# Turning xf ahead of the second branch's high products, and the router's first layer and x1's transposes ahead of its low ones

## What is computed

```
h  = softmax(x xT / 16) x                      # inside each tile
h  = h + xn + circular convolution, decayed scan over time, correlation   (xn = layernorm(h))
xf = layernorm(h)
router: logits = gelu(xf W1r + b) W2r + b      # two of eight experts for each row
twice: ctx = [x, v]; shared and two routed experts: gelu(ctx w1 + b) w2 + b -> gates, halt
refined = gelu(x2 r1 + b) r2 + b
out = h + xf + weight * refined
```

## Time and profile before

| | us |
|---|---|
| median of 3 runs | 774.84 (774.31 to 776.21) |
| the profiled execution | 774.78 |
| its span, first to last instruction | 773.0 |

### The profile page before, as it was taken

The page is one execution under the profiler, slowest core; times in us unless marked ns, Lnnn a source line. Parts: engine busy times, 40 slices in busy tenths (PEclk is TensorE's granted clock), DMA queues, the critical chain, the costliest instruction groups (busy, mean ns, idle before and its releaser), DMA issues.

```text
span 773.0 us, 14304 instructions
## 1 busy us (share of the span) xinstructions
PE 728.1 (94%) x4516; PEld 615.8 (80%) x4516; DVE 610.8 (79%) x1430; ACT 569.3 (74%) x1359; POOL 372.1 (48%) x438
## 2 busy tenths in 40 slices
PE   5757999999999999999999999999999999999986
PEld 3646778888888888888888888888888888888875
DVE  4847778978978878878878878879789789789662
ACT  4665778787787787887887886887887887877663
POOL 1426446445555555545545555454564564463310
PEclk9688999999999999999999999999999999999997
DMA  8300000000000000000000000000000000000000
GB/s 326 123 15 1 8 0 12 10 21 3 19 22 2 21 21 3 20 22 0 22 22 1 22 22 1 21 22 1 22 21 1 8 8 2 8 8 1 8 8 14
DMA packets 11611, 17.27 MB, mean 22 GB/s; under 512 B 1232, under 2 KB 10504, under 8 KB 11024
## 3 DMA queue, kind: packets, MB, share of 16 engines
q1 hardware_dynamic: 11536, 16.35, 6.2%
HBM read 13.20 MB, written 3.15 MB: 21 GB/s over the span
## 4 chain that ended last, share of the span: by engine, by line
PE 66%; ACT 15%; DVE 12%; issue 5%; POOL 1%; DMA 1%; SPq 0%; POOLq 0%; ACTq 0%; DVEq 0%
PE ctl L495 23%; PE ctl L511 10%; PE ctl L472 5%; PE ctl L501 4%; PE ctl L514 4%; ACT L906 4%; ACT L1060 3%; DVE both L1324 3%; DVE work L1319 3%; PE cd L472 3%; PE cd L666 3%; PE ctl L481 3%; ACT work L909 2%; DVE both L1325 2%; PE ctl L482 2%
## 5 line engine op out<-in xcount | busy, mean ns | idle before, releaser
L375 POOL TENSOR_TENSOR hm_lo<-gl,mexp 128x256 fp32r<-128x256 f32 x144 | 127.8, 913 | 124.2 <-DVE gl L1256 120.7
L495 PE MATMUL ctl<-w2e_hi,hm_hi 128*128 128x512 f32 (+1 forms) x432 | 160.9, 382 | 0.1
L495 PE MATMUL ctl<-w2e_lo,hm_hi 128*128 128x512 f32 (+1 forms) x432 | 150.3, 360 | 0.0
L965 ACT ACTIVATE work<-ctl 128x256 f32<-128x256 f32 (+1 forms) x144 | 70.2, 487 | 68.6 <-PE ctl L514 59.1
L1242 DVE TENSOR_TENSOR hm_hi<-ge,mexp 128x256 fp32r<-128x256 f32 x144 | 88.7, 631 | 20.0 <-ACT ge L946 17.7
L495 PEld LDWEIGHTS ctl<-w2e_hi,hm_hi 128*128 128x128 f32 x432 | 82.1, 190 | 24.7 <-DVE hm_hi L1242 8.0
L511 PE MATMUL ctl<-w2e_hi,hm_lo 128*128 128x512 f32 (+1 forms) x432 | 100.0, 357 | 0.0
L495 PEld LDWEIGHTS ctl<-w2e_lo,hm_hi 128*128 128x128 f32 x432 | 82.3, 191 | 10.5
L511 PEld LDWEIGHTS ctl<-w2e_hi,hm_lo 128*128 128x128 f32 x432 | 74.6, 188 | 13.6 <-POOL hm_lo L375 0.2
L381 POOL TENSOR_TENSOR rg_lo<-rg,rg_hi 128x512 fp32r<-128x512 f32 x23 | 37.7, 1639 | 70.8 <-ACT rg_hi L902 70.8
L967 ACT ACTIVATE work<-ctl 128x256 f32<-128x256 f32 x144 | 54.5, 378 | 0.0
(11 more groups left out here) (211 smaller groups left out, 2040.3 us busy)
## 6 DMA issues: line engine op xcount, KB each, us to landing
work<-params_dram SPq DMA_DIRECT2D x3, 1152.0 KB, 13.2
xT<-turned_dram SPq DMA_DIRECT2D x24, 128.0 KB, 2.2
out_dram<-y SPq DMA_DIRECT2D x24, 128.0 KB, 1.7
xa<-x_dram SPq DMA_DIRECT2D x16, 128.0 KB, 2.2
par<-params_dram SPq DMA_DIRECT2D x1, 1280.0 KB, 10.9
work<-params_dram SPq DMA_DIRECT2D x2, 512.0 KB, 11.2
xa<-x_dram SPq DMA_DIRECT2D x8, 119.0 KB
par<-params_dram SPq DMA_DIRECT2D x1, 512.0 KB, 16.0
```

The lines of the kernel that those rows point to most:

```text
L375: TT(hm[1][:, j, c, :], gl[:, c, part, :], pairs(tile, j, c), ALU.mult).then_inc(done, 1)
L495: mm(dst[:, a:z], hm[0][:, j, c, :], w2e[i][:, c, a:z], start=(c == 0 and i == 0), stop=False)
L965: AF(tan[tile.s][:, 1:kinds, j, :], ctl_t[:, D:kinds * D].rearrange("p (a d) -> p a d", a=kinds - 1), ACT.Tanh, scale=0.5)
```

## The change

Only the order of steps in two `slot` functions changes; no instruction is added or removed, and every step keeps its own waits.

On PE, xf's transposes (L686 in the new numbering) come directly behind `refine_in(o)`, ahead of `expert_hi` of the second routed branch. The router's first layer and `turned(n)` then come ahead of `expert_end` and `expert_lo` of that branch. On ACT, the two copies of xf come ahead of `refine_units(o)`, and the two copies of x1 ahead of `unit(t, 2)`.

```diff
@@ PE's slot @@
                 if o.exists() and t.exists():
                     refine_in(o)
 
+                if f.exists():
+                    passed(pe, xf_v, f)
+                    for q in range(KD):
+                        last = nc.tensor.transpose(pd[:, q * P:(q + 1) * P], xf[f.s][:, q * P:(q + 1) * P], ident)
+                    last.then_inc(xfT_ps, 1)
+
                 if t.exists():
                     passed(pe, hm1_v, t, per=3)
                     passed(pe, u1_sb, t, per=BR, step=1)
                     if t.low == 0:
                         pe.wait_ge(set_dve, 3)
                     expert_hi(ctl[0], 1, t, hm1_v, 0, 2 * D)
-
-                if f.exists():
-                    passed(pe, xf_v, f)
-                    for q in range(KD):
-                        last = nc.tensor.transpose(pd[:, q * P:(q + 1) * P], xf[f.s][:, q * P:(q + 1) * P], ident)
-                    last.then_inc(xfT_ps, 1)
-
-                if t.exists():
-                    expert_end(ctl[0], 1, t, en1_v, 2 * D)
-                    expert_lo(ctl[0], 1, t, hl1_g, eb1_sb, u1_ps, 2 * D)
 
                 if f.exists():
                     passed(pe, xfT_sb, f)
...
                     turned(n)
+
+                if t.exists():
+                    expert_end(ctl[0], 1, t, en1_v, 2 * D)
+                    expert_lo(ctl[0], 1, t, hl1_g, eb1_sb, u1_ps, 2 * D)
 
                 if f.exists():
                     passed(pe, rh_sb, f)
@@ ACT's slot @@
                     unit(t, 1, u1_sb, u1_ps, ctl[1], 2)
 
+                if f.exists():
+                    passed(act, e_ps, f, back=1, per=2)
+                    passed(act, rh_ps, f, back=1)
+                    passed(act, xfl_g, f, back=1)
+                    state(xfT, pd, D, f, xfT_ps, xfT_sb)
+                    state_hi(1, pd, f, xfh_sb, f)
+
                 if o.exists():
...
                     refine_units(o)
 
                 if f.exists():
-                    passed(act, e_ps, f, back=1, per=2)
-                    passed(act, rh_ps, f, back=1)
-                    passed(act, xfl_g, f, back=1)
-                    state(xfT, pd, D, f, xfT_ps, xfT_sb)
-                    state_hi(1, pd, f, xfh_sb, f)
                     passed(act, rh_ps, f)
                     AF(rh[:, :], pd[0:HID, 0:P], ACT.Gelu, bias=pv("b1r", HID)).then_inc(rh_sb, 1)
...
-                if t.exists():
-                    unit(t, 2, u1_sb, u1_ps, ctl[0], 2)
-
                 if n.exists() and t.exists():
...
                         state_hi(0, pc, n, x1h_sb, f)
+
+                if t.exists():
+                    unit(t, 2, u1_sb, u1_ps, ctl[0], 2)
```

## The result

The changed kernel takes 792.57 us (median of 4 runs, 789.78 to 793.13); the kernel before, on the same chip, 774.58 (4 runs, 772.30 to 776.21). The ratio is 1.0227 (95% interval 1.0191 to 1.0263): 18 us slower, where 9.6 were forecast, and above the range. The profiled execution took 792.92 us, its span 791.1, the mean granted clock 0.974 as before.

A forecast was written before the change was run, and what follows sets the result against it. PE was busy for 94% of the span; the slot's end was taken as set by ACT and DVE, PE's path some 0.2 us shorter. 774.8 + 5.0 (middle slots) + 3.1 (first slots) + 1.5 (clock) = 784.4 us, range 778.8 to 789.8.

The forecast's parts named there:

- rival (a): Whole kernel: slower, as worked out, 784.4 us with a range of 778.8 to 789.8; chance 0.82.
- the stall: PE at xf's transposes, middle slots: free at 390.66, it waits for DVE's xf until 391.27, 0.61 us idle.
- Rival (b): PE at xf's transposes: faster, 771.4 us, as PE begins the high products during the wait for xf; chance 0.04.
- The step that failed: DVE's routing steps behind L717: 0.44 us later, held to be outside the chain of waits, which goes over ACT.
- rival (d): Much slower, 794 us: POOL's `rg_lo` late for PE, or table loads pushed further, 0.5 us a slot more; chance 0.07.
- +0.25 a slot: Middle slots: PE's way grows by 0.44 - 0.19, ACT's by 0.11, so PE is later; 20 slots, +5.0 us.
- the wait at L481 should be nearly gone: PE at L481, before `sab`: a sign expected in the changed profile; PE's 0.19 us there is given back.
- rival (c): No change: PE's loss is given back where it meets DVE or ACT, as at L481; 776.5 us; chance 0.07.
- The first slots: Slots of tiles 0 to 2: high products come behind the wait for xf; together +3.1 us, from +2 to +3.5.
- one fall: PE's clock in tiles 1 and 2: one longer idle gap brings half speed, +1.5 us; none to two, 0 to +3.5.

The follow-up runs named there:

- experiment 6: Parts of the change alone in the kernel before: only xf's transposes early, 793.09 us; only low products and `unit(t, 2)` late, 790.70; only ACT's new order, 795.40.
- experiment 1: Changed kernel with POOL's u0 and `vu` subtractions ahead of its two additions into `base`: 783.85 us, ratio 1.0108 to the kernel before.
- experiment 8: Changed order from tile 3 on only, with POOL's u0 and `vu` ahead of `base`: 779.41 us, ratio 1.0050 to the kernel before.
- experiment 4: Changed kernel with the new order only from tile 3 on, tiles 0 to 2 keeping the old one: 785.56 us, ratio 1.0124 to the kernel before.
- experiment 2: Kernel before with POOL's u0 and `vu` ahead of `base`: 775.87 us, ratio 1.0000.
- experiment 5: Changed kernel with xf's transposes behind four of the six high products instead of ahead of all: 788.72 us, ratio 1.0185 to the kernel before.
- experiment 3: Kernel before with one more 128x128 addition, its result unused, on POOL in each slot: 779.52 us, ratio 1.0039.

## Why the prediction was right and wrong

**Right:** slower (rival (a)), with the stall it named. The transposes start at 6.94 us where PE was free at 6.34: 0.60 for the 0.61 forecast. The waits at L686 are 15.7 us in 24 slots (some 13 forecast), those of L717 for `rh` are gone, ACT idles ahead of the copies of xf. Rival (b) fell: PE held the high products behind the transposes that waited, in every slot. `rg_hi` and POOL's `rg_lo` are early enough, as worked out; L381 takes even less (1295 ns for 1639): before, it stands beside DVE's L1314 (392.44 to 393.39) in tile 12 and takes 1.69, after, beside no DVE instruction, 1.29.

**The step that failed** is the sentence "DVE's routing steps begin 0.44 later with L717; they were not in the chain of waits, which goes over ACT." They are what POOL's four instructions wait for, and these shut out DVE's product on the way to `sab`. That made 0.31 of the slot's 0.49, 6 us. The measured time is close to rival (d)'s 794, but by luck: the half of (d) that named a later table load was not it (the load is 0.18 later, near the 0.11 forecast), and PE did not wait for `rg_lo`. The collision could be read from before: POOL's L425 took 1.45 us next to 0.74 for its twin L421, and DVE's L1324 1.11 next to 0.69 for L1325. I looked at POOL only for what PE waits for.

**The term "+0.25 a slot".** PE's steps came to 4.42 for the forecast 4.27: 0.19 from the transposes to the first high product (0.13 forecast) and 0.32 from L514 to L717 (0.25). So L562 is 0.58 later (0.44). But more could be given back than 0.19. I had taken 0.58 for the pitch from L742 to L481, and 0.36 is possible (experiment 6), so at least 0.41 was to spare there (0.77 - 0.36), and 0.15 more at `hm_hi` (10.68 from L481 to the next slot before, 10.53 after). PE's own way therefore ends at 29.54 at most and does not set the slot. What does, once the sum no longer meets POOL, is ACT's way, with DVE's as long: 0.18 for the 0.11 forecast, as `unit(t, 2)` waits for the later L514. So the 0.25 was near the 0.18 that experiments 1 and 8 show, but it was put on the wrong engine, and that is luck. With the collision it is 0.49: 9.7 us for the forecast 5.0.

**The end of the slot in the kernel before.** I took the 0.17 us of idle time at L481 for ACT's and DVE's one way. They are two, and the later one passes through `hm_hi`. This is why "the wait at L481 should be nearly gone" failed (7.5 us in 23 waits), and why rival (c), which looked for all that is given back at L481, looked in one of two places.

**The first slots.** +3.1 and one fall, +1.5, were forecast; measured +6.8, and 7.0 by experiment 4. Tile 0 has +1.34 (1.15), tile 2 0.97 without its fall (0.98). The second fall, 1.5, was in the range of the term. Tile 1's +3.0 is 1.0 for the order, 1.5 for its fall and 0.5 for the longer slow stretch at its start, which no term had.

**The sum:** 5.0 + 3.1 + 1.5 were forecast, 9.7 + 6.8 came, and 1.5 ahead of tile 0 that the order doesn't explain. The range ended at 789.8, with 0.40 a slot as its upper bound; 0.49 with the collision is beyond that, and experiment 1, where the sum doesn't meet POOL, is inside with 783.85. One sum of the prediction is wrong in itself: rival (c) with 0.1 a slot and +1 gives 774.8 + 2 + 1 = 777.8, not 776.5; this changes no other number.

## What to carry to other kernels

Ask of every step that moves not only who waits for it, but which instructions of DVE and POOL will then stand side by side: two instructions of one shape on one engine that differ in length (1.45 and 0.74, 1.11 and 0.69) mark a collision that no wait shows. Idle time ahead of a matmul can be missing as well: whether it waited is told by its start against the end of what it needs. Before costing an order, write the slot as the largest of its ways, each with its margin; two such sums did it here, and they showed that the smallest edit (one step of ACT moved ahead of another) was worth more than a new order. A wait taken away where another way is as long gives nothing (experiments 2 and 5).

## What the runs showed of the hardware

- **DVE and POOL shut each other out for the rest of an instruction.** DVE's product of 128x768 took 0.96 to 1.43 us; in the middle slots of thirteen of the fourteen kernels that was what was left of POOL's instruction when the product began, plus 0.81 to 0.83 (0.17, 0.60, 0.52 and 0.60 left in the kernel before, the changed one and experiments 1 and 3). In the fourteenth (experiment 6, low products late) 0.07 was left and the product took 0.96, as long as in the slots where no POOL instruction runs beside it. So the first 0.15 us or so of the product run beside POOL, and only the rest is shut out. The sum of 128x512 takes 0.69 alone and 1.11 with 0.56 left. POOL's instruction of 0.73 us becomes 1.45 when DVE is ahead of it. Neither shows as waiting: the time stands in the instruction.
- **A matmul that waits holds those behind it**, though their operands are there: in 24 of 24 slots the high products began only behind the waiting transposes.
- **Equal gaps, unequal clock:** 2.42 us of idle PE in the same slot, once with and once without a fall to 1.2 GHz.
